# Tokens and sort in one block: a later branch and Gelu in the token loop, half of the low one-hots on GpSimd, the first chunk gathered before the experts' block

## What is computed

```python
x = _layernorm(x + attention(x))                       # gives x2
probs = softmax(flat @ gate_W); topk_w, topk_idx = top_k(probs, 2); topk_w /= topk_w.sum()
out = 0.5 * gelu(flat @ shared_W + shared_b)
for e in range(8):
    h = gelu(flat @ W1[e] + b1[e])
    out = out + combine[:, e:e + 1] * (h @ W2[e] + b2[e])
x = _layernorm(x + _layernorm(out) * gamma + beta)
```

## Time and profile before

| | us |
|---|---|
| runs, median of 3 | 1937.59 (1936.98 to 1939.03) |
| the profiled execution, its own time | 1924.92 |
| its span in the profile | 1923.1 |
| TensorE busy | 1813.5 (94%) |
| VectorE busy | 1342.4 (70%) |
| ScalarE busy | 1050.6 (55%) |
| GpSimd busy | 354.3 (18%) |

### The profile page before, as it was taken

The page is one execution under the profiler, slowest core; times in us unless marked ns, Lnnn a source line. Parts: engine busy times, 40 slices in busy tenths (PEclk is TensorE's granted clock), DMA queues, the critical chain, the costliest instruction groups (busy, mean ns, idle before and its releaser), DMA issues. The chain is left out here.

```text
span 1923.1 us, 31681 instructions
## 1 busy us (share of the span) xinstructions
PE 1813.5 (94%) x11161; PEld 1217.2 (63%) x11161; DVE 1342.4 (70%) x1772; ACT 1050.6 (55%) x1554; POOL 354.3 (18%) x399
## 2 busy tenths in 40 slices
PE   7999999999999999999999999778858999999986
PEld 5555555555555555555555554577747999999982
DVE  5787777777777787777777778655575666666646
ACT  5555555655555565555555555454544555555537
POOL 1000000000000000000000000011116677777664
PEclk9999999999999999999999999898878999999998
DMA  5000000000000000300000000344232333433435
GB/s 169 17 28 18 22 17 28 23 17 28 17 23 20 26 23 17 113 17 23 23 22 23 17 23 17 117 159 154 99 113 42 93 81 88 88 87 87 88 51 175
DMA packets 67091, 110.30 MB, mean 57 GB/s; under 512 B 7713, under 2 KB 41697, under 8 KB 64673
## 3 DMA queue, kind: packets, MB, share of 16 engines
q1 hardware_dynamic: 48704, 81.48, 12.5%
q0 software_dynamic: 18272, 27.31, 7.1%
HBM read 70.20 MB, written 38.57 MB: 57 GB/s over the span
## 5 line engine op out<-in xcount | busy, mean ns | idle before, releaser
L435 ACT ACTIVATE a_e<-banks 128x1024 f32<-128x1024 f32 x512 | 490.3, 1025 | 388.1 <-PE banks L326 388.1
L544 DVE TENSOR_TENSOR a_esum<-a_esum,a_e 128x1024 f32<-128x1024 f32 x384 | 469.9, 1224 | 33.7 <-DVE a_esum L544 0.9
L340 PE MATMUL banks<-a_e,a_v 128*64 128x512 f32 x2048 | 481.6, 602 | 0.0
L340 PEld LDWEIGHTS banks<-a_e,a_v 128*64 128x64 f32 x2048 | 130.0, 136 | 252.0 <-issue 228.2
L541 DVE TENSOR_TENSOR a_esum<-a_e 128x1024 f32<-128x1024 f32 x64 | 78.5, 1226 | 250.0 <-ACT a_e L435 250.0
L326 PE MATMUL banks<-a_qh,a_kh 64*128 64x512 f32 x1024 | 223.6, 431 | 5.3 <-issue 5.3
L63 POOL MEMSET ident<- 128x128 f32 x1 | 0.2, 206 | 1196.4 <-POOLq L109 1196.4
L548 DVE RECIPROCAL a_inv<-banks 128x512 f32<-128x512 f32 x64 | 214.4, 3350 | 1.2 <-PE banks L351 1.2
L326 PEld LDWEIGHTS banks<-a_qh,a_kh 64*128 64x128 f32 x1024 | 96.8, 184 | 173.5 <-issue 132.2
L326 PE MATMUL banks<-a_ql,a_kh 64*128 64x512 f32 x1024 | 203.9, 392 | 0.0
L326 PE MATMUL banks<-a_qh,a_kl 64*128 64x512 f32 x1024 | 203.5, 391 | 0.0
(11 more groups left out here) (227 smaller groups left out, 3243.6 us busy)
## 6 DMA issues: line engine op xcount, KB each, us to landing
attn_out<-a_ot SPq DMA_DIRECT2D x64, 256.0 KB, 2.0
a_w<-w_qkv SPq DMA_DIRECT2D x32, 256.0 KB, 3.2
raw<-attn_out SPq DMA_DIRECT2D x4, 2048.0 KB, 8.2
t_ot<-attn_out SPq DMA_DIRECT2D x4, 2048.0 KB, 7.9
raw<-w_up SPq DMA_DIRECT2D x8, 1024.0 KB, 5.1
raw<-w_down SPq DMA_DIRECT2D x8, 1024.0 KB
raw<-x_t SPq DMA_DIRECT2D x8, 512.0 KB, 9.3
x_rows<-x POOLq DMA_DIRECT2D x7, 512.0 KB, 3.3
```

The costliest lines, as they stand in the source:

```text
L340: mm = pe.matmul(o_acc[h * DH:(h + 1) * DH, :], v[quad % 2][:, n, head], e[(slot * ST + n) % NE][:, h * BANK:(h + 1) * BANK], start=n == 0 ...
L435: act.activation(e[t % NE], ring[n % RING], ACT.Exp, scale=SCALE).then_inc(e_ok, 1)
L544: dve.tensor_tensor(acc[:, :], acc[:, :], e[(slot * ST + n) % NE], ALU.add).then_inc(add_ok, 1)
```

## The change

Tokens and routing become one block.
- *Steps of the loop.* Tile n is turned at step n + 5 up to tile 23, then 24 and 25 at step 29, 26 and 27 at 30, 28 and 29 at 31, 30 and 31 at 32. `branch(n)` stands at the step of turn n + 1, behind `project` and ahead of the turn; `branch(27)` (EARLY) stands ahead of `project(31)`. `gelu(n)` stands one step behind its branch. VectorE does `inverse` first in a step. Parts are tiles 0-7, 8-15, 16-27, 28-31; `top` is divided over two steps, ranks come three steps behind the last branch of a part, places four. ScalarE takes its first splits ahead of everything as before; VectorE too, with its constants behind `add(0)`.
- *Low one-hots.* They are now products of comparison and 64 + number of the pair, one instruction a tile: for parts 0 and 1 on GpSimd (32), for the rest on VectorE (24 and 8). The labelled product and its third column go; the number is read out of the marked sum by a reciprocal, and ROUND. 160 columns instead of 252.
- *Last part.* Ranks and totals of tiles 28 to 31 come from matmuls over the chosen one-hots (`last_rank`, `totals`) instead of GpSimd's counts.
- *First gather.* GpSimd gathers chunk 0 at the end of the block, once the target rows are there; the other columns of `numbers` follow on VectorE. The low part of the first up weights moves to the head of VectorE's part of `experts`; the identity is kept.

The diff, cut to its core (allocations, imports of names and the removed body of `routing`, which the new lines repeat, are left out):

```diff
+    SORTS = [slice(0, 16), slice(32, 48), slice(16, 32), slice(48, 56), slice(56, 64)]
+    MARK = CH
...
-    PARTS = [range(0, 8), range(8, 16), range(16, 24), range(24, 30), range(30, TT)]
+    PARTS = [range(0, 8), range(8, 16), range(16, TT - 4), range(TT - 4, TT)]
+    LAST = len(PARTS) - 1
+    MOST = max(len(part) for part in PARTS)
+    EARLY = {TT - 5: TT - 1}
...
-        turns = {}
-        for n in range(TT):
-            at = GROUPS[group_of[n]][-1] + LAG
-            while at in turns and at < TT:
-                at += 1
-            turns.setdefault(min(at, TT), []).append(n)
-        branch_step = {n - 1: t for t in range(TT + 1) for n in turns.get(t, []) if n}
-        branch_step[TT - 1] = TT
+        turn_at = {n: n + 5 if n < TT - 8 else TT - 3 + (n - TT + 8) // 2 for n in range(TT)}
+        last_turned = {t: [n for n in range(TT) if turn_at[n] == t] for t in range(TT + 1)}
+        branch_step = {n: EARLY.get(n, turn_at[n + 1] if n + 1 < TT else TT) for n in range(TT)}
...
-            return [n for n in range(TT - 1) if branch_step[n] == t]
+            return [n for n in range(TT) if branch_step[n] == t and n not in EARLY]
+        def gelus_after(t):
+            return [n for n in range(TT) if branch_step[n] + (n not in EARLY) == t]
+        def branched_before(t):
+            return [n for n in EARLY if EARLY[n] == t]
...
+            def lows(p):
+                gp.wait_ge(low_ok, p + 1)
+                for j in range(TOPK):
+                    for t in PARTS[p]:
+                        gp.tensor_scalar(low_hot[:, j, t, :], counting[:, :], low[:, j, t:t + 1], float(MARK + j * TT + t),
+                                         ALU.is_equal, ALU.mult).then_inc(lows_ok, 1)
...
             for t in range(TT + 1):
                 for k, group in enumerate(GROUPS):
                     if min(group[-1] + 1, TT) == t:
                         store_rows(k)
-                for p in range(len(PARTS)):
-                    if tops[p] == t:
+                for p in range(LAST):
+                    if tops[p] + (p < LAST - 1) == t:
                         count(p)
-                while stored < len(GROUPS) and branch_step[GROUPS[stored][-1]] <= t:
+                    if p < LAST - 1 and tops[p] + 4 == t:
+                        lows(p)
+                while stored < len(GROUPS) and (branch_step[GROUPS[stored][-1]] < t or t == TT):
                     store_shared(stored)
                     stored += 1
+            gp.wait_ge(rows_out, 16 * len(GROUPS))
+            gp.wait_ge(numbers_ok, 1)
+            for a in range(CT):
+                gp.indirect_dma_start(out=xg[0][:, a, :], out_offset=None, in_=x2_rows,
+                                      in_offset=bass.IndirectOffsetOnAxis(ap=numbers[:, 0, 0, a:a + 1], axis=0))\
+                  .then_inc(xg_in[0], 16)
...
+            def last_rank():
+                pe.wait_ge(hot_ok, LAST + 1)
+                start, n = PARTS[LAST][0], len(PARTS[LAST])
+                pe.matmul(ranks(LAST), before[:, :], flat(chosen, LAST), start=True, stop=False)
+                for t in range(n):
+                    mm = pe.matmul(banks[6 + LAST % 2][:, (start + t) * E:TT * E], ones[:, :],
+                                   (cum[:, start, :] if t == 0 else chosen[:, start:TT - t, :]).rearrange(
+                                       "p a b -> p (a b)") if t else
+                                   cum[:, start, :].unsqueeze(1).to_broadcast([P, n, E]), start=False, stop=t == n - 1)
+                mm.then_inc(rank_done, 1)
+            def totals():
+                pe.wait_ge(r_done, TT)
+                start = PARTS[LAST][0]
+                pe.matmul(banks[0][:, 0:E], ones[:, :], cum[:, start, :], start=True, stop=False)
+                for t in range(start, TT):
+                    mm = pe.matmul(banks[0][:, 0:E], ones[:, :], chosen[:, t, :], start=False, stop=t == TT - 1)
+                mm.then_inc(totals_ok, 1)
...
+            pe.wait_ge(consts_ok, 2)
             for t in range(TT + 1):
+                for n in branched_before(t):
+                    branch(n)
                 if t < TT:
                     project(t)
+                for n in branched_after(t):
+                    if turn_at[n] < t:
+                        branch(n)
+                if t == TT:
+                    rank(LAST - 1)
                 for n in turned_after(t):
                     turn(n)
-                    if n:
-                        branch(n - 1)
-                for p in range(len(PARTS)):
-                    if tops[p] + 1 == t:
+                for n in branched_after(t):
+                    if turn_at[n] == t:
+                        branch(n)
+                for p in range(LAST - 1):
+                    if tops[p] + 3 == t:
                         rank(p)
-            branch(TT - 1)
-            for p in range(len(PARTS)):
-                if tops[p] + 1 > TT:
-                    rank(p)
-            pe.wait_ge(r_done, TT)
-            pe.matmul(banks[0][:, 0:E], ones[:, :], cum[:, TT, :], start=True, stop=True).then_inc(totals_ok, 1)
+            last_rank()
+            totals()
+            pe.wait_ge(lows_ok, early_lows)
+            sort(0)
+            sort(1)
...
+                    gelu(n)
+                for n in turned_after(t) if t >= TT - 1 else ():
+                    copy_turned(n)
                 if ends_group(t) is not None:
                     deviation(ends_group(t))
-            gelu(TT - 1)
+            for n in gelus_after(TT + 1):
+                gelu(n)
+            act.wait_ge(gap_ok, 1)
+            act.activation(e2[:, :], gap[:, :], ACT.Exp).then_inc(e2_ok, 1)
+            for part in range(len(SORTS)):
+                these = SORTS[part]
+                act.wait_ge(ones_ok, part + 1)
+                act.activation(high_hot[:, these, 0, :], high_hot[:, these, 1, :], ACT.Identity, scale=own[:, :])\
+                   .then_inc(own_ok, 1)
+            act.wait_ge(up_in, 16)
+            act.copy(up_h[:, :], up[:, :]).then_inc(up_h_ok, 1)
+            act.wait_ge(w_turned, 1)
+            act.copy(w_t[:, :], banks[3][0:CH, 0:P]).then_inc(w_t_ok, 1)
         @block.vector
         def _(dve):
                 dve.tensor_tensor(pre[n % 2][:, :], banks[4 + n % 2][:, 0:D], sbias, ALU.add).then_inc(pre_ok, 1)
...
+                        link(ins)
+                        dve.tensor_tensor(chosen[:, these, :], hot[:, 0, these, :], hot[:, 1, these, :], ALU.add)\
+                           .then_inc(hot_ok, 1)
             def places(p):
...
+            def constants():
+                dve.wait_ge(consts_ok, 5 + E + PLANNED)
+                dve.tensor_copy(counting[:, :], counting_i[:, :])
+                dve.tensor_copy(own[:, :], own_i[:, :])
+                dve.tensor_copy(spare[:, :, :], spare_i[:, :, :])
+                dve.memset(plan[:, NEW, 0:1], 1)
+                dve.memset(numbers[:, NCHUNK:, 0:2, :], 0)
+                for buffer in (nch, ends[0], ends[1]):
+                    ins = dve.memset(buffer[:, 0:E], 0.0)
+                link(ins)
...
             for t in range(TT + 1):
+                if t and ends_group(t - 1) is not None and t < TT:
+                    inverse(ends_group(t - 1))
                 if t + 2 < TT:
                     ot_low(t + 2)
+                for n in branched_before(t):
+                    biased(n)
+                    top(LAST - 1)
                 if t < TT:
                     add(t)
                     statistics(t)
-                if t and ends_group(t - 1) is not None:
-                    inverse(ends_group(t - 1))
-                for n in branched_after(t):
-                    biased(n)
-                    if t == TT and n - branched_after(t)[0] < TOPK and tops[2] + 2 < TT:
-                        lows(2, n - branched_after(t)[0])
-                    if t == TT and n in (part[-1] for part in PARTS):
-                        top([part[-1] for part in PARTS].index(n))
+                if t == 0:
+                    constants()
                 if ends_group(t) is not None:
                     moments(ends_group(t))
-                if t < TT:
-                    for p in range(len(PARTS)):
-                        if tops[p] == t:
-                            top(p)
-                        if tops[p] + 2 == t:
-                            places(p)
-                        for j in range(TOPK):
-                            if p < 2 and tops[p] + 3 + j == t:
-                                lows(p, j)
-            biased(TT - 1)
-            top(len(PARTS) - 1)
-            for p in range(3, len(PARTS)):
-                places(p)
-                for j in range(TOPK):
-                    lows(p, j)
-            dve.nop().then_inc(keep["lows_ok"], 1)
...
+                for p in range(LAST - 1):
+                    if tops[p] in (t, t - 1):
+                        top(p, (t - tops[p],))
+                    if tops[p] + 4 == t:
```

(35 more changed lines are left out.)

314 lines of the change are left out of this document (124 added, 190 removed).

## The result

The changed kernel takes 1889.95 us (median, 1885.24 to 1891.84); on the same chip the kernel before took 1938.24 (1936.98 to 1939.03). The ratio is 0.9748, with a 95% interval of 0.9728 to 0.9768: 48 us faster, where 54.9 were predicted. The time predicted, 1882.7, is 7 us too low. The profiled execution took 1888.51 us, span 1886.8.

A forecast was written before the change was run, and what follows sets the result against it. Between attention and experts, where TensorE is full, 233 us hold TensorE waits for normalization, GpSimd's counts and ScalarE-VectorE exchanges. Token steps and start 43.4 plus tail 11.5 make 54.9 us: 1937.6 - 54.9 = 1882.7 us, range 1875 to 1902.

The forecast's parts named there:

- The start: First block before add(0): VectorE begins with the low part of w_o instead of constants, 3.2 us earlier.
- the loop: Token steps from add(0) to add(31): 124.4 us against 164.6, a gain of 40.2 us.
- the tail: Start of project(31) to first expert matmul: 46.8 us instead of 58.3, a gain of 11.5 us.
- Two signs of being right: Token steps: no TensorE idle behind x2, x2t or counts before tile 27.
- Group wait and ring: Token steps: TensorE waits for each four-tile group's normalization; ScalarE and VectorE wait on each other through Gelu, bias and split.
- rivals 1 and 2: Token steps: part of the normalization wait stays, 1897 us, chance 0.22; or ScalarE-VectorE waiting stays, 1903, chance 0.06.
- rival 2: Token steps: mutual waiting of ScalarE and VectorE stays, groups remain about 20 us instead of 15.9; 1903 us, chance 0.06.
- hidden up to 13 us: Token steps: next half's load lands 9.4 us after issue, needed after four projections (15.9 us), so it costs nothing.
- GpSimd's products: Token steps: 32 low one-hot products of parts 0 and 1, 0.3 to 0.6 us each, cost 0.
- Rival 3: Token steps: GpSimd products wait for VectorE subtracts, so count(2) and rank(2) come 16 us later; 1899 us, chance 0.05.
- lie beside the landing: Before the experts: block boundary (0.3 to 1.8 us) and w_up's low part (2.3) end by S+46.1, hidden beside gather(0)'s landing.
- Rival 4: Token steps: TensorE runs at the lower clock (1.2 GHz) throughout, +122 us, so 2005 us; chance 0.03.

## Why the prediction came out as it did

The mechanism and the forecast's case held; the gain forecast was 7.5 us too high, 47.4 at the first up product for 54.9. The start gave 0.4 more than forecast, the loop 3.0 less and the tail 5.0 less. The tail was the part sized worst: on its own clock it gave 6.5 us of the 11.5. By steps, S being the start of project(31), at 1353.0:

- **Start**, 3.2 predicted: from ScalarE's first cast to add(0) 12.32 us before, 8.69 after, so 3.6.
- **Loop**, 124.4 predicted up to add(31), 128.5 measured. One microsecond is add(31) behind top(2), which the tail's clock had. Of the other 3.0, 1.2 are branches, which wait 3.8 us where I had 2.6: 1.54 for branch(27) where I had 2.0, 1.28 and 0.24 for the two that follow their own turn where I had 0.3 each, and 0.74 for the late load, which I hadn't. Rank(1) waits 0.45. The rest, 1.4, I didn't trace. Two signs of being right were not met by these waits: TensorE was idle for counts and for x2t before branch(27), though for 0.45, 0.74 and 1.28 us only.
- **One sentence of the prediction was wrong**: the branch does not move a step behind its turn. Branch(n) stood at the step of turn n + 1 before as well; only their order within the step changed. What moved was the inverse, the Gelu and the ranks, and the runs price them, each taken back alone, at 11.5, 7.9 and 16.2 us of loop. The "later branch" of the title rests on the same slip. The sum didn't hang on it.
- **Group wait and ring** (rivals 1 and 2): gone. The kernel with the order back (+24.3) shows what rival 2 described: its turns that wait for x2 follow each other 21 us apart, where rival 2 had 20.
- **Loads** were called hidden up to 13 us. They land 9.4 and 10.7 us behind their issue (medians), and still casts wait 17.1 us for them. The prediction measured from a load's issue to the projection that needs the tile; the cast stands two steps ahead of that. The cast that waited longest could have started at 1326.1, some 7 us behind the issue of the two loads (1318.4 and 1318.9, SyncE's queue), and started at 1331.5. The cast's lead hid nearly all of these waits from TensorE.
- **GpSimd's products**: 0.88 us on average for 0.3 to 0.6. The cost, 0, stood, as it would have up to 1.4 us each. The row that I leaned on was a chain of 8-column sums; 128 columns are another size. Rival 3 had the blocking right, but it strikes three products of the 16 that were looked at: the longest takes 1.74 us, the median 0.71. The Trainium skill (SBUF — State Buffer, "Who interferes with whom") has that rule, and the trace agrees.
- **VectorE's products**: 24 in 4.79, so 0.20 us each; I had 0.15, the estimate by the Trainium skill (VectorE: DVE Perf Modes, "The TRN2 errata") was 0.22. The distance behind a single cast was the wrong row. From start to start of what follows, 24 products took 4.7 us for 3.6 and 8 took 1.6 for 1.2, so 1.5 us in all, 1.1 of it ahead of the plan.
- **The tail** came to S+51.8 for S+46.8. At the plan it was 1.2 late (products); sorted came at S+39.5 for 36.8, since the sorts behind ScalarE's last multiplication ended 2.6 us after it where I allowed 1.3 (the granted clock is 0.65 from 1388 to 1393); numbers to gather was 0.9 for 0.2; gather to turn 5.2 for 4.2; turn to up 3.5 for 2.65. **The step that failed** in the tail is the sentence that the block boundary and w_up's low part "lie beside the landing". The boundary waits for GpSimd's last issue (1398.37) and 2.9 us more, so the turn starts at 1401.3, 1.0 us later than the 4.24 of the earlier trace rows would have it; then the subtract of 2.29 us stands ahead of the rows' split on VectorE, 0.85. Together 1.9 us.
- **The distance of profile and median**, 12.7 us: the profile of before has the busy share in its experts of the chips on which before takes 1924 to 1926 us, the runs the time of the others. On one chip the difference of the medians is 48.3 us, near the 47.4 of the first up product.

Rival 4, a low clock in the loop, did not occur (1.00). In the tail the clock was low, and keeping it up there was worth 1.7 to 3.4 us of tail, though no time of the kernel.

## What to carry to other kernels

Where several engines pass each tile on in every step, put what another engine waits for at the head of the step and what nobody waits for a step later; here two such moves gave 21 us of loop with no work removed, and taking back the later ranks alone cost 16. Cost a small instruction by a row of its own size, and cost a block boundary by who issues last into it. A subtract of 2.3 us on VectorE must not be placed beside a gather that GpSimd has on the critical chain: here that cost 1.8 us of issue. And where a tail moves by 1 to 2 us with the clock, judge an edit by the stretch it changes and by the kernel's time, not by the tail of one profile.

## What the hardware did that I had not expected

- A gather's issue on GpSimd takes 1.04 us alone and 2.79 to 2.93 us beside a VectorE subtract of two SBUF inputs (2.28 us). I knew this of sums (1.23), not of a gather's issue. Placing the subtract at the end of the block cost 0.9 us from the numbers to the first up product for this reason, where it was to win 0.9.
- The same program has 1 to 2% more idle time on TensorE in the experts on one chip than on another, at the same granted clock: 10 us of 1925.
- 52 unread transposes behind the sort held the clock at 1.00 up to 1400; the turn behind 3.27 us of idleness still took 0.63 us where it takes 1.09 in the changed kernel; the up products 2.88 us later took as long as there (0.58, then 0.21 apart), at a granted clock of 0.50.
